# Attention row maxima over 64-query blocks of both heads of a pair, in a fused transformer-layer kernel

## What is computed

```python
qkv = x @ Wqkv + bqkv                       # 16 heads of 16 channels
att = einsum('bhqd,bhkd->bhqk', q, k) * 16 ** -0.5
att = softmax(where(causal, att, -inf))     # 512 queries x 512 keys
x = layernorm(x + einsum('bhqk,bhkd->bhqd', att, v) @ Wout + bout)
h = silu(x @ w1.T * s1) * (x @ w2.T * s2)   # ternary weights, 256 -> 1024
h = gelu(h @ h1.T * sh1)
h = gelu(h @ h2.T * sh2)
return layernorm(x + h @ w3.T * s3)         # 1024 -> 256
```

## Time and profile before

| | us |
|---|---|
| median of 3 runs | 2168.27 |
| profiled execution: span | 2166.8 |
| PE busy in it | 2118.4 (98%) |
| ACT busy | 1316.1 (61%) |
| DVE busy | 1259.9 (58%) |
| POOL busy | 492.9 (23%) |
| DMA queue of SP, share of 16 engines | 28.6% |

### The profile page before, as it was taken

The page is one execution under the profiler, slowest core; times in us unless marked ns, Lnnn a source line. Parts: engine busy times, 40 slices in busy tenths (PEclk is TensorE's granted clock), DMA queues, the critical chain, the costliest instruction groups (busy, mean ns, idle before and its releaser), DMA issues.

```text
span 2166.8 us, 52048 instructions
## 1 busy us (share of the span) xinstructions
PE 2118.4 (98%) x16294; PEld 1878.8 (87%) x16294; DVE 1259.9 (58%) x3928; ACT 1316.1 (61%) x2807; POOL 492.9 (23%) x899
## 2 busy tenths in 40 slices
PE   8789999999999999999999999999999999999998
PEld 4368889989889888899989889988999898988998
DVE  7765555556555565556556565565556556565452
ACT  6456566666556666566666666666566666656553
POOL 2222122221222222122221122222122132122220
PEclk9889999999999999999999999999999999999999
DMA  8742332232322332332232322333232232321100
GB/s 275 239 120 63 77 71 70 61 81 64 90 65 61 82 74 69 75 69 73 61 81 64 90 64 62 81 76 73 71 76 70 56 82 69 83 64 37 37 6 10
DMA packets 95940, 167.69 MB, mean 77 GB/s; under 512 B 19204, under 2 KB 38404, under 8 KB 95672
## 3 DMA queue, kind: packets, MB, share of 16 engines
q1 hardware_dynamic: 91912, 152.75, 28.6%
q10 hardware_dynamic: 3760, 11.54, 1.5%
HBM read 98.26 MB, written 68.17 MB: 77 GB/s over the span
## 4 chain that ended last, share of the span: by engine, by line
PE 89%; DVE 1%; DMA 0%; issue 0%; SPq 0%; ACT 0%; POOL 0%; POOLq 0%; DVEq 0%
PE ring L1241 44%; PE ring L1226 10%; PE pM L1116 7%; PE pS L1104 6%; PE pO L1164 6%; PE ring L1254 5%; PE ring L1176 4%; PE ring L1206 2%; PE ring L1196 2%; PE ring L1148 1%; PE ring L1215 1%; DMA qk_d<-c 0%; SPq L614 0%; DVE full_g L960 0%; DMA Qs<-nm 0%
## 5 line engine op out<-in xcount | busy, mean ns | idle before, releaser
L921 DVE CUSTOM_DVE_ANT_0 pM<-pM,mask 128x512 f32<-128x512 f32 (+3 forms) x1024 | 498.7, 502 | 366.1 <-PE pM L1116 292.3
L1241 PE MATMUL ring<-Yhi,H 128*128 128x256 f32 x1984 | 501.7, 289 | 0.0
L1241 PE MATMUL ring<-Xhi,H 128*128 128x256 f32 x1984 | 497.9, 288 | 0.0
L1241 PE MATMUL ring<-Ylo,H 128*128 128x256 f32 x1984 | 489.2, 282 | 0.0
L1241 PE MATMUL ring<-Xlo,H 128*128 128x256 f32 x1984 | 486.4, 282 | 0.0
L1241 PEld LDWEIGHTS ring<-Ylo,H 128*128 128x128 f32 x1984 | 377.8, 190 | 7.2 <-issue 3.4
L1241 PEld LDWEIGHTS ring<-Yhi,H 128*128 128x128 f32 x1984 | 377.0, 190 | 7.1 <-issue 3.4
L1241 PEld LDWEIGHTS ring<-Xlo,H 128*128 128x128 f32 x1984 | 379.1, 191 | 0.8
L1241 PEld LDWEIGHTS ring<-Xhi,H 128*128 128x128 f32 x1984 | 378.4, 191 | 1.0 <-issue 0.2
L1116 PE MATMUL pM<-Ks,Qs 128*128 128x512 f32 x992 | 304.2, 340 | 20.6 <-DVE mx L921 9.0
L865 ACT ACTIVATE Yhi<-ring,cols 128x256 fp32r<-128x256 f32 x248 | 117.8, 475 | 266.8 <-PE ring L1241 170.1
(11 more groups left out here) (146 smaller groups left out, 3518.7 us busy)
## 6 DMA issues: line engine op xcount, KB each, us to landing
qk_d<-c SPq DMA_DIRECT2D x120, 256.0 KB, 3.4
Qs<-qk_d SPq DMA_DIRECT2D x120, 192.0 KB
Ks<-qk_d SPq DMA_DIRECT2D x120, 192.0 KB
qk_d<-c SPq DMA_DIRECT2D x120, 128.0 KB, 3.0
xTs<-in_xT SPq DMA_DIRECT2D x16, 512.0 KB, 4.3
raw<-in_h SPq DMA_DIRECT2D x8, 1024.0 KB, 10.4
xz<-in_x SPq DMA_DIRECT2D x16, 512.0 KB, 3.9
H<-raw ACTq DMA_DIRECT2D x8, 1024.0 KB, 9.3
```

Source lines behind the costliest of these rows:

```text
L921: nc.vector.tensor_tensor_reduce(pM[:, h % 2, 0:n], pM[:, h % 2, 0:n], mask[:, T - n:T], 1.0, NEG, ALU.add, ALU.max, mx[:, t, h:h + 1]).th ...
L1241: mm = nc.tensor.matmul(to, w, x_part, start=(k == 0 and m == 0), stop=(k == KB - 1 and m == 1))
```

## The change

The maxima are taken for blocks of 64 queries of both heads of a pair at once. The stationary operand is again 128 columns, now 64 queries of one head and the same 64 of the other, and the keys streamed are those up to the block's end, in steps of 64. To have these 128 columns side by side, `Qs` is laid out pair, block of 64, head, query. There are still 16 maxima steps a group; they stream 4608 columns. Step `max:off:g:t:h` now means pair h % 2, block 2t + 1 for h = 0, 1 and 2t for h = 2, 3. The mask is made for blocks of 64, twice. The transfers that fill `Qs` change with the layout: the queries of a stack are loaded by one transfer for each pair, in runs of 64 elements, and `nm` is moved by eight transfers (pair, head, even or odd block), the first four counted on `nm_in` and the last four on a new semaphore `nm_in1`. PE waits for `nm_in` before unit 0 and for `nm_in1` before unit 2 of `exp`. The tables of the order are as before.

```diff
-        Qs = sb("Qs", [P, 2, PAIRS, 2, T], F32R)
+        Qs = sb("Qs", [P, 2, PAIRS, MB, 2, MQ], F32R)
...
-        def m_cols(t):
-            return (t + 1) * P
+        def m_block(t, h):
+            return 2 * t + 1 - h // 2
+
+        def m_cols(t, h):
+            return (m_block(t, h) + 1) * MQ
...
                         for s in range(2):
                             at = SROWS * s
-                            sp.dma_start(Q[at + NMAX:at + STACK, :, s].bitcast(F32), q_rows[s]).then_inc(landed, 16)
+                            for p in range(PAIRS):
+                                sp.dma_start(Q[at + NMAX:at + STACK, p, :, s].bitcast(F32), q_rows[s][:, p]).then_inc(landed, 16)
                             sp.dma_start(K[at + NMAX:at + STACK].bitcast(F32), k_rows[s]).then_inc(landed, 16)
                             if not first:
-                                sp.dma_start(Q[at:at + NMAX, :, s].bitcast(F32), zero_d).then_inc(landed, 16)
+                                sp.dma_start(Q[at:at + NMAX, :, :, s].rearrange("m p i q -> m (p i) q").bitcast(F32),
+                                             zero_d.rearrange("m p (i n) -> m (p i) n", n=MQ)).then_inc(landed, 16)
...
-                        for j in range(G):
-                            at = SROWS * (j % 2)
-                            sp.dma_start(Q[at:at + 2, j // 2, j % 2].bitcast(F32),
-                                         nm[j:NM_ROWS:G].bitcast(F32)).then_inc(nm_in, 16)
+                        for p, landed in enumerate((nm_in, nm_in1)):
+                            for s in range(2):
+                                to = Q[SROWS * s:SROWS * s + NMAX, p, :, s].bitcast(F32).rearrange("m (t a) q -> m a t q", a=2)
+                                for first in range(2):
+                                    of = nm[2 * first + p:NM_ROWS:G].bitcast(F32).rearrange("m (t s q) -> m s t q", t=TB, s=2)
+                                    sp.dma_start(to[:, 1 - first], of[:, s]).then_inc(landed, 16)
...
                             for p, (landed, n) in enumerate(((nm_in, 64), (nm_done, 1))):
                                 for s in range(2):
-                                    at = 32 * (2 * p + s)
-                                    copy = nc.scalar.activation(Q[SROWS * s:SROWS * s + NMAX, p, s],
-                                                                ring[at:at + NMAX, BANKS[kind, off, a]], ACT.Copy)
+                                    to = Q[SROWS * s:SROWS * s + NMAX, p, :, s].rearrange("m (t a) q -> m a t q", a=2)
+                                    for first in range(2):
+                                        at = 32 * (2 * first + p)
+                                        of = ring[at:at + NMAX, BANKS[kind, off, a]].rearrange("m (t s q) -> m s t q", t=TB, s=2)
+                                        copy = nc.scalar.activation(to[:, 1 - first], of[:, s], ACT.Copy)
...
                             pe.wait_ge(nm_in, (b * NG + g + 1) * 64)
-                        elif steps is HEAD and u == 2:
-                            pe.wait_ge(nm_done, b * NG + g + 1)
+                        elif u == 2:
+                            if steps is HEAD:
+                                pe.wait_ge(nm_done, b * NG + g + 1)
+                            else:
+                                pe.wait_ge(nm_in1, (b * NG + g + 1 - HEAD_MAXIMA) * 64)
...
-                                                  Q[:, p, first:last + 1, kt * P:T], start=True, stop=True)
+                                                  Q[:, p, 2 * kt:MB, first:last + 1].rearrange("k i s q -> k s i q"), start=True, stop=True)
...
-                        nc.tensor.matmul(pM[:, h % 2, 0:n], Q[:, h // 2, h % 2, t * P:(t + 1) * P],
-                                         K[:, h // 2, 0:n], start=True, stop=True).then_inc(m_ready, 1)
+                        nc.tensor.matmul(pM[:, p, 0:n], Q[:, p, m_block(t, h)].rearrange("k s q -> k (s q)"),
+                                         K[:, p, 0:n], start=True, stop=True).then_inc(m_ready, 1)
```

More of the change, by code:

```diff
@@ L44 @@
 TB = T // P
+MQ = P // 2
+MB = T // MQ
 HALF = T // 2
@@ L339, in build @@
         Kx = over(nc, xlo_at, "Kx", [P, 2, PAIRS, T], F32R)
-        Qx = over(nc, y_at, "Qx", [P, 2, PAIRS, 2, T], F32R)
+        Qx = over(nc, y_at, "Qx", [P, 2, PAIRS, MB, 2, MQ], F32R)
         cx = over(nc, x1_at, "cx", [P, 2, 2, T], F32R)
@@ L399, in build @@
         picked_q, picked_k, head_in, picks, zeros_in = map(sem, ("picked_q", "picked_k", "head_in", "picks", "zeros_in"))
-        qk_saved, nm_in, o_moved = map(sem, ("qk_saved", "nm_in", "o_moved"))
+        qk_saved, nm_in, nm_in1, o_moved = map(sem, ("qk_saved", "nm_in", "nm_in1", "o_moved"))
         stack_in = [sem(f"stack_in{n}") for n in range(2)]
@@ L417, in build @@
         TABLES = sum(kind == "table" for kind, _, _ in STEPS)
+        HEAD_MAXIMA = sum(kind == "neg_max" for kind, _, _ in HEAD)
         HEAD_TABLES = sum(kind == "table" for kind, _, _ in HEAD)
         SAVES = 16 * 4
-        LOADS = 16 * 6
+        LOADS = 16 * 8
         HEAD_COPIES = 3
-        N_CONSTS = 13
+        N_CONSTS = 15
         def need(eng, s, n):
@@ L596, in move @@
                         held(sp)
-                        q_rows, k_rows = (qk_d[g, n * G * D:(n + 1) * G * D].rearrange(
-                            "(p s d) r n -> s (d r) p n", p=PAIRS, s=2) for n in range(2))
+                        q_rows = qk_d[g, 0:G * D].rearrange("(p s d) r (i n) -> s (d r) p i n", p=PAIRS, s=2, n=MQ)
+                        k_rows = qk_d[g, G * D:2 * G * D].rearrange("(p s d) r n -> s (d r) p n", p=PAIRS, s=2)
                         for s in range(2):
                             at = SROWS * s
-                            sp.dma_start(Q[at + NMAX:at + STACK, :, s].bitcast(F32), q_rows[s]).then_inc(landed, 16)
+                            for p in range(PAIRS):
+                                sp.dma_start(Q[at + NMAX:at + STACK, p, :, s].bitcast(F32), q_rows[s][:, p]).then_inc(landed, 16)
                             sp.dma_start(K[at + NMAX:at + STACK].bitcast(F32), k_rows[s]).then_inc(landed, 16)
                             if not first:
-                                sp.dma_start(Q[at:at + NMAX, :, s].bitcast(F32), zero_d).then_inc(landed, 16)
+                                sp.dma_start(Q[at:at + NMAX, :, :, s].rearrange("m p i q -> m (p i) q").bitcast(F32),
+                                             zero_d.rearrange("m p (i n) -> m (p i) n", n=MQ)).then_inc(landed, 16)
                     elif kind == "neg_max":
@@ L670, in _ @@
                 pool.wait_ge(consts, 11 + s)
-            tri = mask[:, T - P:T]
-            nc.gpsimd.affine_select(out=tri, in_=tri, compare_op=ALU.is_ge, fill=NEG, base=0,
-                                    pattern=[[-1, P]], channel_multiplier=1).then_inc(consts, 1)
+            tri, upper = mask[:, T - MQ:T], mask[0:MQ, T - MQ:T]
+            nc.gpsimd.affine_select(out=tri, in_=tri, compare_op=ALU.is_ge, fill=NEG, base=-MQ,
+                                    pattern=[[-1, MQ]], channel_multiplier=1).then_inc(consts, 1)
+            pool.wait_ge(consts, 13)
+            nc.gpsimd.memset(upper, 0.0).then_inc(consts, 1)
+            pool.wait_ge(consts, 14)
+            nc.gpsimd.affine_select(out=upper, in_=upper, compare_op=ALU.is_ge, fill=NEG, base=0,
+                                    pattern=[[-1, MQ]], channel_multiplier=1).then_inc(consts, 1)
             pool.wait_ge(consts, N_CONSTS)
@@ L745, in work @@
                             at = SROWS * s
-                            nc.scalar.activation(Q[at:at + STACK, :, s], pS[at:at + STACK], ACT.Copy).then_inc(head_in, 1)
+                            nc.scalar.activation(Q[at:at + STACK, :, :, s], pS[at:at + STACK].rearrange("k p (i q) -> k p i q", q=MQ), ACT.Copy).then_inc(head_in, 1)
                         act.wait_ge(picked_k, g + 1)
@@ L784, in work @@
                         need(act, nm_in, (b * NG + g) * 64)
+                        need(act, nm_in1, (b * NG + g - HEAD_MAXIMA) * 64)
                         nc.scalar.activation(nm[:], ring[0:NM_ROWS, BANKS[kind, off, a]], ACT.Copy).then_inc(nm_done, 1)
@@ L1109, in iteration @@
                         g, t, h = a
-                        n = m_cols(t)
+                        n, p = m_cols(t, h), h % 2
                         Q, K = stacks(steps, off, g)
```

2 lines of the change are left out of this document (1 added, 1 removed).

## The result

| | before | changed |
|---|---|---|
| median of the runs, us | 2169.45 (2166.58 to 2173.18, 4 runs) | 2219.16 (2218.61 to 2220.02, 4 runs) |
| ratio of the times | | 1.0232, 95% interval 1.0220 to 1.0243 |
| span of the profiled execution, us | 2166.8 | 2217.9 |
| mean granted clock of TensorE | 0.991 | 0.986 |

The change makes the kernel 50 us slower, 2.3%. It was predicted slower, but at 2175 with a range up to 2198, so the time lies above the whole range. (A fourth run of the kernel before has joined the three that were known when the prediction was made.)

The account below looks back on a forecast made before the run. PE, busy 98% of the span, was taken to bound the kernel. The terms -11.5 + 7 + 11 + 0 gave +6.5 us on the 2166.8 us span, 2173; the runs' median, 1.5 higher, made it 2175 us, range 2156 to 2198.

Parts of the forecast that it names:

- Saves late: Saves of `qk:1:1` queue behind eight `nm` issues on SP, 1.3 us later; PE loses 0.5 a time, 14 iterations, +7 us.
- `Osb` late: Transfers out of `Osb` follow `nm` on SP, delaying ACT's tanh; PE loses 0.8 us a time, 14 iterations, +11 us.
- The price of an issue: Each `nm` issue on SP takes 0.625 us, from 0.37 to 0.68 possible; eight take 5.0 us, 2.5 more.
- dearer issues: Rival: at 0.68 us an issue on SP, eight take 5.4, both chains 0.45 longer, 2192 us in all; chance 0.20.
- Columns: Maxima matmuls on PE stream fewer columns, saving 0.18 us a group over 64 groups, -11.5 us.
- Unit 0 at no cost: The first four `nm` issues serve pair 0, so unit 0 of `exp` on PE sees no change: 0.
- Stack loads at no cost: Two more load issues a stack on SP, 0.7 us, and more packets stay hidden before that stack's first maxima: 0.
- The head, -2 to +2, taken 0: From 40 to 130 us, DVE's shorter maxima against ACT's eight half-length copies a group and longer stack loads: taken 0.
- Strided operand at no cost: PE reads the moving operand of `exp` in runs of 64 elements with gaps: taken 0, with no row showing it.

Follow-up runs that it names:

- e1: The change with four 2x8x64 transfers of the maxima in place of eight of 2x4x64, half the maxima at other queries: 2176.44 us, ratio 1.0037.
- e5: The kernel before with only the change's column counts and mask, leaving the last 64 keys out of two heads' maxima: 2163.11 us, ratio 0.9983.
- e6: e1 with the column counts of the kernel before, so the new layout alone: 2186.61 us, ratio 1.0083.
- e10: e6 with the maxima written to the stack in 2 KB runs instead of 256-byte runs, landing at wrong queries: 2181.65 us, ratio 1.0056.
- e7: e1 with the stack loads of before, six issues with 2 KB runs, queries in wrong places: 2173.53 us, ratio 1.0027.
- e15: e14 with the stack loads of before too, leaving of the layout only PE's operand in runs of 64: 2170.31 us, ratio 1.0013.
- e14: e10 with the head's copies on ACT as before, four of 512 columns a group instead of eight of 256: 2176.85 us, ratio 1.0042.
- e8: The kernel before with each stack's query load split in two, one per pair, still 2 KB runs: 2169.32 us, ratio 1.0005.
- e3: The change with pair 1's four transfers of the maxima issued by POOL instead of SP: 2224.66 us, ratio 1.0251.
- e4: The change with pair 1's four transfers of the maxima issued by ACT instead of SP: 2276.41 us, ratio 1.0493.
- e11: The kernel before with two transfers of the maxima, both pairs at once, in place of four: 2167.46 us, ratio 0.9995.

## Why the prediction was wrong

The direction and both mechanisms stood in it; the size did not. The predicted excess was 6.5 us, the measured 50. Two things failed: the size of the two waits (18 us in the sum, 41 measured) and the terms of the layout that were taken at 0 (without the four added issues the sum has -11.5, and e1 measured +8.5). By its own steps:

- **Saves late, +7 (0.5 a time).** This is the first step that failed. From e1 to the changed kernel the sections of the program that hold this wait grew by 1.6 us a time, 22 us in all. The step took the saves as 1.3 us late with eight issues in 5.0 us; the eight take 5.44 and the saves leave 1.8 late, and PE loses 1.1 us in most iterations. The rest is four iterations with a late landing or a long issue, one of them with a fall of the clock behind it. The reading also rested on an unusual iteration: in that of the earlier trace rows at 727.45 one of the four saves (L536) was such a long issue, 1.62 us.
- **`Osb` late, +11 (0.8 a time).** The second: 1.4 a time, 19 us. The estimate had 2.5 us more, a landing of 1.2 and 0.3 in hand. The landing was right (949.32 to 950.50); the eight issues add 2.9, and PE loses 1.0 in one kind of iteration, taken at 0.3, and 1.6 in the other, taken at 1.1. Two iterations with a long issue and a fall of the clock lost 4.1 each.
- **The price of an issue, 0.625.** It is 0.68 (5.44 us for eight), the upper bound of the prediction. The rival "dearer issues" named it, with both chains 0.45 us longer: 12.6 us in 28 places, about half of the 23 that the two waits are above the sum. The other half is in the long issues, the late landings and the clock, for which no term stood in it. The rival's own time, 2192, is 27 us short.
- **Columns, -11.5.** Too large: by the distances over two steps it is some 8 us, and e5 measured 4 (2 to 6). The distance to the next start, 0.06 behind 128 columns, was read as the cost of the step; it leaves out the 0.055 us by which the step behind the successor is longer. The prediction set it against the rule of the Trainium skill (TensorE: Matmul & The Clock Gate, section LDWEIGHTS) of 107 ns for a load of 128 columns. The trace agrees with the rule: such loads start 108 ns or more apart, and the gain of about 9 us that the prediction worked out by it was the better number.
- **Unit 0 at no cost.** Wrong by 5 us (e6 to e10): the four transfers that it waits for take 0.70 us each from start to start in short runs of 2x8x64, not 0.63, and less than 0.1 of it was in hand. In the changed kernel itself, in rows of 2x4x64, they take 0.67.
- **Stack loads at no cost.** Wrong by 3 (e7) to 6.5 us (e15). The two more issues were priced at 0.33 to 0.35, but each query issue costs 0.6 and each of the `Ks` loads 0.2 more than it did: a stack's loads take 5.2 to 6.1 us in place of 3.2. Two thirds of the loss are before 200 us (PE's wait for the last load of a stack, `pM` for `Qs<-zero_d`, grows from 5.0 to 8.0 us in the head), one third in the loop.
- **The head, -2 to +2, taken 0.** The copies cost between 2 us (the trace) and 5 (the medians, e14), which are not clear of each other. DVE's shorter maxima gave the head no more than a microsecond (in e5's profile the first copy of `nm` of the loop comes 1.0 us earlier).
- **Strided operand at no cost.** Right (e15).

Why a landing of the saves mostly takes 2.6 us and now and then 3.9, and why single issues last a microsecond longer, stays open. So does the loss of some 3 us behind 1900 us, which e1, e6, e7 and e10 have and e14 and e15 have in part.

## What to carry over

On a queue that only issues transfers, count the issues that stand ahead of the first transfer that is waited for: four more there cost 43 to 50 us here, two more elsewhere (e8) nothing. Read the price of an issue from a transfer of the same shape and runs: a stack's query load costs 0.34 us as one transfer, 0.39 for each half with 2 KB runs (e8) and 0.62 for each half with short ones. Read the reserve in every iteration and not in one or two: the usual ones give the cost, and the few with a long issue, a late landing or a fall of the clock can double it. And read what a short matmul costs over two steps, not to the next start. A gain of a few tenths of a microsecond a group does not pay for a longer row of transfers, and moving that row to another engine's queue (e3, e4) pays with that engine's own order.

## What the runs showed of the hardware

- A matmul of 64 columns with 128 weight columns is followed by the next after 31 ns (median), one of 128 after 61, but the step after that is as much longer: loads of 128 weight columns start at least 102 ns apart and nearly always 108 (11,333 pairs), and 128, 192 and 256 columns all take 236 to 240 ns over two steps.
- Issuing on SP, medians from start to start in a row: maxima 2x512 0.63 us, 2x8x64 0.70, 2x4x64 0.67, two heads' maxima in one (e11) 0.76; 16x512 out of `Osb` 0.63. A query load of 48x2x512 from DRAM lasts 0.34, the half of it in runs of 64 (48x8x64) 0.57 to 0.62. Fewer, larger issues are the cheap ones.
- Behind waits of PE of 1.96, 2.14 and 2.21 us the granted clock was 1.2 GHz for 3.4 us each, and PE got 21 matmuls done in 4 us in place of 34.
- Runs of 256 bytes cost the DMA engines no more time. The changed kernel moves the same bytes in nearly twice the packets, and the queue's share is lower, also when multiplied by the longer span (572 us against 620):

```profile
DMA packets 185575, 167.74 MB, mean 76 GB/s; under 512 B 121300, under 2 KB 140500, under 8 KB 185304
...
q1 hardware_dynamic: 181544, 152.76, 25.8%
```

  Before there were 95940 packets, 19204 of them under 512 B, and a share of 28.6%. The Trainium skill (DMA: Bandwidth & Descriptors, section Specifications) wants 512 B for line rate; the trace shows no loss with runs below it, but no run here had the queue's rate as its limit. The cost of the short runs was in issuing them.
